# One program for the attention and the feed-forward stage of an adaLN block on one memory map, with the last attention block and the first feed-forward block interleaved

## What is computed

```python
x = x + ga * attn(layernorm(x) * (1 + ca) + sa)
x = x + gb * ffn(layernorm(x) * (1 + cb) + sb)

# attn: 4 heads of 128, gated linear attention with a sign-flipping decay
q = silu(h @ wq); k = sigmoid(h @ wk); v = h @ wv; f = 1 - k
S = S * f + k v^T        # per step and head;  out = q S
out = layernorm(out * sigmoid(h @ wg1 @ wg2)) * norm_w
return out @ wo

# ffn
xr = mu_r * h + (1 - mu_r) * h_prev;  xk likewise      # h_prev: one row back
r = sigmoid(xr @ W_r.T);  k = square(relu(xk @ W_k.T))
return r * (k @ W_v.T)
```

## Time and profile before

| | |
|---|---|
| median of three runs | 1960.5 us (1958.51 to 1961.96) |
| profiled execution, its own time | 1956.89 us |
| span from its first to its last instruction | 1955.0 us |
| mean granted TensorE clock | 0.99 |
| busy: PE, DVE, ACT, POOL | 97%, 75%, 35%, 25% |
| HBM read and written | 47.72 and 33.55 MB |

### The profile page before, as it was taken

One profiled execution on the slowest core, in us unless ns is written; L12 is line 12 of the kernel. 1 busy time (PEld: TensorE's weight loads), 2 busy tenths in 40 slices (PEclk: granted clock), 3 DMA queues, 4 the chain that ended last, 5 costly groups with the idle time before them and its releaser, 6 DMA issues. The chain is left out here.

```text
span 1955.0 us, 53550 instructions
## 1 busy us (share of the span) xinstructions
PE 1894.0 (97%) x23233; PEld 1665.9 (85%) x23233; DVE 1464.8 (75%) x2900; ACT 687.7 (35%) x1279; POOL 496.1 (25%) x536
## 2 busy tenths in 40 slices
PE   5799999999999999999999999996999999999998
PEld 1688999889998999889988999885788888888887
DVE  4377677766777677767777677766899999999996
ACT  2233333333333333333333333331544344334432
POOL 2101121111111121112111121111245444544454
PEclk9899999999999999999999999998999999999999
DMA  6100011000100001000100010001211111111110
GB/s 247 65 2 24 24 32 37 24 23 24 45 24 24 23 34 35 23 23 24 46 24 23 23 40 29 24 13 50 71 65 50 60 65 65 54 55 65 65 55 33
DMA packets 42624, 84.69 MB, mean 43 GB/s; under 512 B 2308, under 2 KB 2840, under 8 KB 42392
## 3 DMA queue, kind: packets, MB, share of 16 engines
q1 hardware_dynamic: 38008, 73.42, 10.8%
q10 hardware_dynamic: 4384, 7.87, 1.1%
HBM read 47.72 MB, written 33.55 MB: 42 GB/s over the span
## 5 line engine op out<-in xcount | busy, mean ns | idle before, releaser
L148 POOL TENSOR_TENSOR ln_rs<-ln_ve,mhalf 128x2 f32<-128x2 f32 x64 | 73.5, 1149 | 986.7 <-DVE ln_ve L143 986.7
L700 DVE TENSOR_TENSOR Tot<-Tot 128x256 f32<-128x256 f32 (+2 forms) x192 | 47.2, 246 | 155.8 <-PE lvl L924 100.4
L844 PE MATMUL bank<-hT_hi,wq_hi 128*128 128x256 f32 x512 | 152.2, 297 | 10.0 <-POOL hT_lo L486 10.0
L154 DVE TENSOR_SCALAR xn<-xs,ln_mv,ln_rs 128x512 f32<-128x512 f32 x128 | 132.0, 1073 | 32.2 <-POOL ln_rs L148 32.2
L844 PE MATMUL bank<-hT_hi,wk_hi 128*128 128x256 f32 x512 | 150.4, 294 | 0.0
L792 DVE TENSOR_TENSOR og<-bank,og 128x512 f32<-128x512 f32 x64 | 44.3, 692 | 138.0 <-PE bank L1007 138.0
L844 PE MATMUL bank<-hT_lo,wq_hi 128*128 128x256 f32 x512 | 146.2, 286 | 0.0
L844 PE MATMUL bank<-hT_hi,wq_lo 128*128 128x256 f32 x512 | 146.0, 285 | 0.0
L1294 PE MATMUL bank<-xk_hi,fk_hi 128*128 128x256 f32 x512 | 144.3, 282 | 0.6 <-DVE xk_lo L1228 0.6
L844 PE MATMUL bank<-hT_lo,wk_hi 128*128 128x256 f32 x512 | 143.8, 281 | 0.0
L1294 PE MATMUL bank<-xk_hi,fk_lo 128*128 128x256 f32 x512 | 143.7, 281 | 0.0
(11 more groups left out here) (196 smaller groups left out, 5806.9 us busy)
## 6 DMA issues: line engine op xcount, KB each, us to landing
xs<-in_L_attn_x SPq DMA_DIRECT2D x32, 512.0 KB, 3.8
x_scratch<-xs SPq DMA_DIRECT2D x32, 512.0 KB, 2.9
xs<-x_scratch SPq DMA_DIRECT2D x32, 512.0 KB, 3.6
out<-xs SPq DMA_DIRECT2D x32, 512.0 KB, 2.8
mod_raw<-in_L_wmod SPq DMA_DIRECT2D x4, 1024.0 KB, 11.7
ffn_raw<-in_L_wmod SPq DMA_DIRECT2D x2, 1024.0 KB, 24.1
raw_q<-in_L_attn_wq ACTq DMA_DIRECT2D x1, 1024.0 KB, 9.5
raw_k<-in_L_attn_wk ACTq DMA_DIRECT2D x1, 1024.0 KB, 14.5
```

Of the source, the lines that this page charges most:

```text
L148: pool.tensor_tensor(out=ln["rs"][:, :], in0=ln["ve"][:, :], in1=mhalf[:, :], op=ALU.pow).then_inc(ln["rstd"], 1)
L154: last = dve.tensor_scalar(ln["xn"][:, ch, :], chunk(ln, n, ch), ln["mv"][:, ch, 0:1], ln["rs"][:, ch:ch + 1], ALU.subtract, ALU.mult)
L700: dve.tensor_tensor(out=Tot[:, off2:off2 + cnt2], in0=t[:, :, 0], in1=t[:, :, 1], op=ALU.mult)
L844: last = pe.matmul(dst, lhs(a, s), rhs(b, s), start=(t == 0), stop=(t == len(terms) - 1))
```

## The change

1. `setup` stays a Block; `attend` and `ffn` become one Block, `blocks`. Every tile has a fixed address (`at`), and tiles of the feed-forward stage lie over attention tiles that are done by then (xk32 over K0, h2 over hF, the split weights over wq, wk, wv). One set of layer norm tiles and semaphores serves both stages.
2. The host transposes W_r, W_k, W_v, so PE turns no weights. ACT casts each as a whole (`weight_high`), POOL forms the low part as a whole (`weight_low`), over 128x2048. W_k is cast in block 30, W_r just after it, W_v in the crossing. W_v is loaded by SP in block 30.
3. `crossing` replaces attention block 31 and the first feed-forward block: the `xk` products (`fk_rows`) and one `xr` product (`fr_rows`) of feed-forward block 0 stand between levels 4 and 7 of block 31; the rest, and the `xk` products of feed-forward block 1, surround its output and its `wo_rows`. The transposes for feed-forward block 0 move into block 30. In the crossing `xk_lo` and `xr_lo` of block 0 are formed by POOL.
4. `flags` and the ticks go. A batch's first block takes no product with S, its last block neither turns nor uses chunk 1's keys. Affine vectors are held per batch, not per block. The wait of the last level for `stat` goes.
5. The last block is stored in two halves.

In the diff the functions `crossing` are, in this order, POOL's, ACT's, DVE's and PE's.

```diff
+                def weight_low(name):
+                    pool.wait_ge(fw_hi[name], 1)
+                    pool.tensor_tensor(out=F[name][1][:, :, :], in0=raw[name][:, :, :], in1=F[name][0][:, :, :].bitcast(F32),
+                                       op=ALU.subtract).then_inc(fw_lo[name], 1)
...
+                def low(m, name):
+                    part, full, hi_s, lo_s = (xk, xk32, xk_hi, xk_lo) if name == "k" else (xr, xr32, xr_hi, xr_lo)
+                    pool.wait_ge(hi_s, m + 1)
...
+                for n in range(LAST):
+                    attention_body(n)
+                weight_low("k")
+                weight_low("r")
+                crossing()
...
+                def crossing():
+                    rstd_o(LAST - 1)
+                    low(0, "k")
+                    low(0, "r")
+                    weight_low("v")
+                    add(LAST - 1, 0)
+                    ln_rstd(pool, ln, mhalf, NB + 1)
+                    add(LAST - 1, 1)
+                    for ch in range(NC):
+                        gate_b(0, ch)
+                    rstd_o(LAST)
...
+                def weight_high(name):
+                    act.wait_ge(raw_in[name], 16)
+                    act.wait_ge(mm[{"k": "q", "r": "k", "v": "v"}[name]], 2 * NB)
+                    act.copy(F[name][0][:, :, :], raw[name][:, :, :]).then_inc(fw_hi[name], 1)
...
+                def crossing():
+                    n, par = LAST, LAST % 2
+                    ogt_high(n - 1, 0)
+                    ogt_high(n - 1, 1)
+                    weight_high("v")
+                    high(0, "k")
+                    high(0, "r")
+                    relu_of(0, 0)
+                    spread_diagonal(n)
+                    relu_of(0, 1)
+                    merge_32(n, par)
+                    q_final(n, par)
+                    r_sigmoid(0, 0)
+                    merge_64(n, par)
+                    keys_turned(n, 0)
...
+                def crossing():
+                    n, par = LAST, LAST % 2
+                    diagonal(n, par)
+                    gated_var(n - 1)
+                    level_update(n, par, 1, 1)
+                    ogt_low(n - 1, 0)
+                    ogt_low(n - 1, 1)
+                    shift(0, "k")
+                    level_update(n, par, 2, 2)
+                    level_merge(n, par, 2, 2)
+                    level_update(n, par, 4, 3)
+                    level_merge(n, par, 4, 3)
+                    shift(0, "r")
+                    level_update(n, par, 8, 4)
+                    level_merge(n, par, 8, 4)
+                    wo_scale(n - 1, 0, bank[3])
+                    level_update(n, par, 16, 5)
+                    level_merge(n, par, 16, 5)
+                    wo_scale(n - 1, 1, bank[1])
+                    level_update(n, par, 32, 6)
+                    ln_stats(dve, ln, n + 2)
+                    ln_var(dve, ln, n + 2)
+                    level_update(n, par, 64, 7)
+                    apply_next(n + 2)
+                    square(0, 0)
+                    square(0, 1)
+                    gated(n, 0)
+                    ka_low(0, 0)
+                    ka_low(0, 1)
+                    state_mid(n)
...
+                def crossing():
+                    n, par = LAST, LAST % 2
+                    near_scores(n, par)
+                    pe.wait_ge(h_sb, 1)
+                    t2(n - 1, 1 - par, 0)
...
+                    level_product(n, par, 2)
+                    pe.wait_ge(s_mid, n)
+                    wo_rows(n - 1, 0, bank[3])
+                    level_product(n, par, 3)
+                    wo_rows(n - 1, 1, bank[1])
+                    level_product(n, par, 4)
+                    pe.wait_ge(xk_lo, 1)
+                    pe.wait_ge(fw_lo["k"], 1)
...
+                    fk_rows(0, 0)
+                    fk_rows(0, 1)
+                    level_product(n, par, 5)
+                    pe.wait_ge(kt_sb, kept_before(n))
+                    fk_rows(0, 2)
+                    fk_rows(0, 3)
+                    level_product(n, par, 6)
+                    pe.wait_ge(og_sb, 2 * n)
+                    pe.wait_ge(xr_lo, 1)
+                    fr_rows(0)
+                    level_product(n, par, 7)
...
+                    turn_keys(n, par, 0)
...
+                    output(n, par, 0)
+                    pe.wait_ge(y_sb, 2 * n - 1)
+                    state_step(n, par, 0)
+                    pe.wait_ge(y_sb, 2 * n)
+                    turn_xn(NB + 1, TT)
+                    pe.wait_ge(ka_lo, 2)
+                    pe.wait_ge(fw_lo["v"], 1)
+                    fv_rows(0)
+                    pe.wait_ge(s_mid, n + 1)
+                    fr_rows(1)
+                    pe.wait_ge(og_sb, 2 * n + 1)
+                    output(n, par, 1)
+                    fv_rows(1)
+                    pe.wait_ge(h_sb, 2)
+                    t2(n, par, 0)
+                    pe.wait_ge(xk_lo, 2)
...
+                    fk_rows(1, 0)
+                    fk_rows(1, 1)
+                    pe.wait_ge(relu, 2)
+                    fk_rows(1, 2)
+                    fk_rows(1, 3)
+                    t2(n, par, 1)
+                    wo_rows(n, 0, bank[2])
+                    pe.wait_ge(r_sig, 2)
+                    wo_rows(n, 1, bank[3])
...
+                    if n == LAST - 1:
+                        sp.wait_ge(mm["gate"], 2 * NB)
+                        sp.dma_start(raw["v"][:, :, :], env["W_v"].rearrange("(k p) n -> p k n", p=P)).then_inc(raw_in["v"], 16)
...
-                pool.tensor_tensor(out=tick[:, :], in0=mhalf[:, 0:1], in1=mhalf[:, 0:1], op=ALU.mult).then_inc(ticked, 1)
...
-                    dve.tensor_scalar(S[0][:, :, :], S[0][:, :, :], flags[:, bass.ds(n + 1, 1)], None, ALU.mult).then_inc(s_flag, 1)
...
-                def turn(turns):
...
+                def output(n, par, ch):
+                    from_state = ch > 0 or not fresh(n)
...
+        a = _np.ascontiguousarray(a.T if name in _TURNED else a)
```

More of the change, by code:

```diff
@@ L113, in slot @@
-def slot(n):
-    return bass.ds(n % XS, 1)
-def rows(n):
[L118 to L131, removed]
+        ident = at("ident", [P, P], 0)
@@ L617, in _ @@
+                h_affine(1)
+                for n in range(LAST):
+                    attention_body(n)
+                h2_affine(0, (bank[5], bank[0]))
+                weight_high("r")
+                crossing()
+                for m in range(1, NB):
+                    ffn_body(m)
             @block.vector
@@ new lines, in low, with square @@
+                def low(m, name):
+                    part, full, hi_s, lo_s = (xk, xk32, xk_hi, xk_lo) if name == "k" else (xr, xr32, xr_hi, xr_lo)
+                    dve.wait_ge(hi_s, m + 1)
+                    dve.tensor_tensor(out=part[1][:, :, :], in0=full[:, :, :], in1=part[0][:, :, :].bitcast(F32),
+                                      op=ALU.subtract).then_inc(lo_s, 1)
+                def square(m, pair):
+                    part = rl[:, 2 * pair:2 * pair + 2, :]
+                    dve.wait_ge(relu, 2 * m + pair + 1)
+                    dve.tensor_tensor(out=part, in0=part, in1=part, op=ALU.mult).then_inc(sq, 1)
@@ new lines, in _ @@
+                dve.memset(A[:, :, :], 0.0)
+                ln_stats(dve, ln, 1)
+                ln_var(dve, ln, 1)
+                h_high(0)
+                apply_next(1)
+                for pair in range(2):
+                    q_silu(0, 0, pair)
+                for pair in range(2):
+                    f_signed(0, 0, pair, y[:, 0, :])
+                q_odd(0, 0)
+                g1_low(0)
+                h_high(1)
+                for n in range(LAST):
+                    attention_body(n)
@@ new lines, in state_step, with fk_rows @@
+                def state_step(n, par, ch):
+                    pe.wait_ge(kt_sb, kept(n, ch))
+                    for h in range(H):
+                        last = pe.matmul(bank[3 + ch][:, h * P:(h + 1) * P], Kt[:, ch, h, :], V[par][:, ch, h * P:(h + 1) * P],
+                                         start=True, stop=True)
+                    last.then_inc(mm["ds"], 1)
+                def fk_rows(m, d):
+                    last = product(KK[d // 2][:, (d % 2) * TB:(d % 2 + 1) * TB],
+                                   lambda a, s: F["k"][a][:, s, d * P:(d + 1) * P], lambda b, s: xk[b][:, s, :], KT)
+                    if d % 2:
+                        last.then_inc(mm["fk"], 1)
```

1242 lines of the change are left out of this document (575 added, 667 removed).

## The result

The changed kernel takes 1933.6 us (median of 4 runs, 1932.83 to 1934.33) beside 1959.5 for the kernel before on the same chip: ratio 0.9866, 95% interval 0.9849 to 0.9883, a gain of 23 to 30 us. I had forecast 1949.1, in a range of 1928 to 1957. The profiled execution has a span of 1932.40 us against 1954.95, so 22.5 us have to be found in the trace. The medians lie 25.9 us apart: the profiled execution of the kernel before ran 2.6 us under its median and that of the changed kernel 0.7 us above.

What follows compares the result with a forecast made beforehand. PE bounds the steady blocks, while latency, with PE waiting on DVE and POOL, bounds the crossing. Crossing 7.4, PE work removed 3.1 and ends 0.9 sum to 11.4 us: 1949.1 us, range 1928 to 1957.

Steps and rivals of the forecast that it cites:

- From there both programs run the same PE-bound blocks: From feed-forward block 2 on: steady blocks keep their times, 17.73 us per feed-forward block, so no gain there.
- The crossing: From T, block 31's first score matmul: feed-forward block 2 at T + 87.4 against T + 94.8, gain 7.4 us.
- the walk: Crossing followed engine by engine in program order: level 2 at 11.4, level 6 at 34.6, keys 44.0; trusted to 2 us.
- The exclusion: In the crossing, POOL's long weight subtractions (4.51 us each) block DVE operations with two SBUF inputs for all their length.
- rival A: Crossing: POOL's long operations do not hold DVE off; gain there 26.5, 1930 us; chance 0.25 with the ground towards it.
- Rivals B: Crossing gains nothing: DVE loses further turns to POOL or the clock stays low, 7 us more; 1956.5; chance 0.10.
- D: Crossing: `xk_lo` comes only after level 7, so fk and first fr run behind the keys; T + 96, 1957.7; chance 0.04.
- Rival C: Feed-forward blocks turn DVE-bound, 1.0 us over the slack in each of 30 blocks; slower, 1979; chance 0.05.
- PE work removed: Blocks 0, 15 and 16: transposes, state step and matmuls with S dropped, 0.9, 1.3 and 0.9, sum 3.1 us.
- Tail: End of the kernel: last add loses a tick of 0.19 us, partly overlapped; half-size last store gives 0.35.
- Start: Start of the kernel: the memset of S in front of the statistics goes; 0 to 0.5 us, taken as 0.4.
- the forecast's own range: Whole kernel: 1943 to 1955 us around the forecast, chance 0.56.

Runs made afterwards that it cites:

- c3: The changed kernel with POOL's three feed-forward weight subtractions covering 128 of 2048 columns, low parts left out of the result; ratio 0.9819 to the kernel before.
- c5: The changed kernel with POOL's subtractions for W_k and W_r moved from the crossing into block 30, ACT's two casts likewise earlier; ratio 0.9837 to the kernel before.
- a1: The changed kernel with every tile moved up by 32 bytes; ratio 0.9858 to the kernel before.
- a2: The changed kernel with the split weights alone moved 32 bytes past a multiple of 64; ratio 0.9879 to the kernel before.
- a3: The changed kernel with the split activations alone moved 32 bytes past a multiple of 64; ratio 0.9874 to the kernel before.
- d1: The changed kernel with wq, wk, wg1 and fk moved to distance -32 from their activations, 512-column products kept at 0; ratio 0.9851 to the kernel before.
- c8: The changed kernel with the last block stored whole instead of in halves; 1933.3 us in one run.

## Why the prediction fell short

- **The failed step: "From there both programs run the same PE-bound blocks", and "attention blocks still 39.79 and feed-forward blocks 17.73 us".** The reasoning was that in a block that is all PE only PE work taken away counts. That left out the pitch of the same matmuls, which the memory map sets. It was worth 3.1 + 5.8 us here, some 9 of 22.5. Every weight and activation got a new address in this change, and I asked of the new map only what it overlays. b2, the kernel before with pads alone, shows this as the cause: its periods are worth 28 x 0.08 + 29 x 0.17 = 7.2 us, and its ratio 0.35%, 6.9 us (4.5 to 9.4). Its profiled span is only 5.5 us shorter, since there one late block waited 1.2 us for `xk_lo`.
- **The crossing.** Forecast T + 86.5 to T + 87.4 with the moved transposes counted ahead of T; measured T + 85.0 with 1.09 us ahead of it. The gain of 8.7 against 7.4 is inside the 2 us that I trusted the walk to; that is agreement within what one crossing can tell, since others of the same kernel's order took 82.5 to 83.6 (last section). Every station of it (level 2, level 6, keys) was within 1.1 us.
- **The exclusion, and rival A.** Shown by c3 and c5, and by the rows above. The Trainium skill's rule (SBUF — State Buffer, "Who interferes with whom") agrees with the trace on both sides: the products with two SBUF inputs were held (4.98 and 5.07 us beside 0.69), the operations with one operand in PSUM were not (1.13 and 0.75). `veo`, a scalar operation on 128x2, lasted 2.90 us in place of 0.17; it has one SBUF input, so by the same section it is held only in a two-port mode, and no row here shows its mode. Rival A is out: without exclusion level 2 would have been at T + 4.
- **Rivals B and D** did not occur: fk stood between levels 4 and 6, and block 2 came at 85.0, not after 94. **Rival C** did not either: PE has no wait in the steady feed-forward blocks, whose 17.54 us are all busy.
- **PE work removed**: 3.1 forecast, 3.3 measured, of which 0.3 is the shorter pitch. Block 16 confirms the price of the four matmuls (0.99, of which 0.11 is pitch, against 0.9). Block 0 does not: with the same work in it, it took 39.6 to 40.9 us in the changed kernel and nine of its variants, long where the start was short.
- **Tail**: the term was mis-sized at 0.5; of the 1.12 us the half store is 0.78 (from the last add's end, 3.27 us before, 2.49 now), the shorter pitch in the last block 0.20, the tick 0.14. **Start**: 0.65 against 0.4, but the same start took 86.5 to 88.5 us in the eleven kernels that share it, so neither number can be told.
- The chance of 0.81 for "faster by over 0.2%" stood on the right mechanism in the crossing. That the range of 1928 to 1957 held 1933.6 was luck: its lower end stood there for rival A (1930 us), which did not happen, and the forecast's own range of 1943 to 1955 missed. The gain came out at about twice the forecast (22.5 us in the traces, 25.9 by the medians, against 11.4), and 8.8 us of the surplus is the term that was not there.

## What to carry to other kernels

Where PE is the bound, look at the addresses of both operands of each matmul kind: here 32 bytes between them moved the pitch by 3%, and two kinds of pads in the kernel before (6.9 us) were worth as much as an edit of the schedule (c5, 6 us). When one program's tiles are laid out anew, forecast the pitch as a term of its own, with both signs. Put long GpSimd operations beside VectorE work that reads PSUM, and before the stretch in which VectorE sets the pace, not inside it.

## What was not expected of the hardware

- The pitch of back-to-back f32 matmuls depends on the distance of the streamed and the held operand within 256 bytes, and with opposite sign for two widths: 512 columns 0.2267 us at distance 0 against 0.2325 to 0.2333 elsewhere; 256 columns 0.1198 at 0, 0.1184 at -32, 0.1167 at +32. The Trainium skill (SBUF — State Buffer, "Who interferes with whom") calls TensorE's two read ports independent and says that PE never waits on anyone; a pitch that hangs on the distance of the two operands is not what one would expect by that, though no run here shows that one port waits for the other. What causes it is open: few distances were seen (64 and 32 bytes to either side, 0, 96 and 128), not each for both widths, and only for parts of f32 products.
- The same crossing, instruction for instruction, took 82.5 to 85.0 us in six kernels (the changed one, a1, a2, a3, d1, c8) that differ only in addresses or in the last store. The stretch before and behind the keys of block 31, with TensorE's granted clock third from the end, in the changed kernel and in c8:

```profile
1351.39:1361.39 10.00, 7.76 (x69) 6.09 (x66) 6.42 (x15) 4.25 (x10) 3.20 (x3) 0.67 0.18 60
```

```profile
1352.15:1362.15 10.00, 7.51 (x81) 6.25 (x76) 7.60 (x16) 5.25 (x12) 3.17 (x3) 0.85 0.18 62
```

At 0.67 more of those 10 us are at the lower of the two levels (1.2 instead of 2.4 GHz) than at 0.85; the difference is 1.8 us at the upper level. PE had idled 4.8 us before level 6 in both, and waits 2.2 and 2.5 us before the keys; where the lower level falls relative to such waits is different from one program to the next. That this makes up the whole spread of 2.5 us is likely and not shown.
